# Order of the scores and of the mask on the diagonal of a causal attention kernel

## What is computed

```python
x = x + attention(layernorm(x))      # x: 2 x 2048 x 512
x = x + moe_ffn(layernorm(x))        # 8 experts of width 352, the 2 best of each token, and a shared expert
# attention, 16 heads of width 32:
k_lat = (x @ wk_w + wk_b) @ wkl_w + wkl_b      # latent width 128, then up to heads; v alike
scores = einsum('bhqd,bhkd->bhqk', q, k) / sqrt(32)
scores = where(causal, scores, -inf)
out = einsum('bhqk,bhkd->bhqd', softmax(scores), v)
```

## Time and profile before

| | us |
|---|---|
| median of 3 runs | 2658.76 |
| lowest and highest | 2655.09, 2663.19 |
| the profiled execution, its own time | 2654.73 |
| its span, first to last instruction | 2652.8 |
| mean granted TensorE clock | 0.935 |
| busy: TensorE, its weight loads, VectorE, ScalarE, GpSimd | 2338.7, 1478.8, 1560.3, 1053.6, 999.8 |
| attention (296.51 to 1484.15) | 1187.64 |

### The profile page before, as it was taken

How to read it: one execution, slowest core, us unless ns; L and a number is a source line. 1 busy time by engine, 2 the same in 40 slices (tenths; PEclk the granted TensorE clock), 3 DMA queues, 4 the chain that set the end, 5 groups by cost and what they waited for, 6 DMA issues and landing times. The chain is left out here.

```text
span 2652.8 us, 34530 instructions
## 1 busy us (share of the span) xinstructions
PE 2338.7 (88%) x12088; PEld 1478.8 (56%) x12088; DVE 1560.3 (59%) x3220; ACT 1053.6 (40%) x1928; POOL 999.8 (38%) x592
## 2 busy tenths in 40 slices
PE   5997699999999999999999699999489999999950
PEld 5775344444444444444443377776467777777740
DVE  3664787667676777766674444443645555555535
ACT  2332155565555555555656422221033333333310
POOL 0000067474656566573746633130221111112036
PEclk8998599899999999998999899999589999999975
DMA  3766512213131313322110234341245454545349
GB/s 100 279 234 231 124 28 65 65 49 74 39 81 33 82 31 80 102 65 65 49 47 27 63 105 143 111 143 48 69 151 178 139 171 146 167 154 160 113 157 381
DMA packets 178740, 301.72 MB, mean 114 GB/s; under 512 B 23616, under 2 KB 65728, under 8 KB 178624
## 3 DMA queue, kind: packets, MB, share of 16 engines
q1 hardware_dynamic: 159360, 242.54, 30.1%
q0 software_dynamic: 14656, 49.29, 5.9%
q10 hardware_dynamic: 4608, 8.39, 0.8%
HBM read 199.65 MB, written 100.27 MB: 113 GB/s over the span
## 5 line engine op out<-in xcount | busy, mean ns | idle before, releaser
L832 ACT ACTIVATE b_pt<-b_st 128x512 f32<-128x512 f32 (+3 forms) x1280 | 620.8, 533 | 489.3 <-PE b_st L910 208.3
L773 DVE TENSOR_REDUCE b_mpart<-b_mx 128x1 f32<-128x512 f32 x768 | 510.2, 685 | 209.2 <-PE b_mx L889 207.4
L649 POOL TENSOR_TENSOR b_acc<-b_acc,b_pt 128x1024 f32<-128x1024 f32 (+1 forms) x256 | 593.4, 2344 | 73.3 <-ACT b_pt L832 73.0
L910 PE MATMUL b_st<-b_q,b_k 97*128 97x512 f32 (+2 forms) x1280 | 497.9, 405 | 71.9 <-ACT b_pt L832 57.9
L889 PE MATMUL b_mx<-b_k,b_q 96*128 96x512 f32 (+2 forms) x1280 | 514.5, 418 | 30.7 <-DVE b_mt L781 25.9
L889 PEld LDWEIGHTS b_mx<-b_k,b_q 96*128 96x128 f32 x1280 | 250.4, 197 | 306.7 <-DVE b_mpart L773 138.6
L910 PEld LDWEIGHTS b_st<-b_q,b_k 97*128 97x128 f32 x1280 | 244.2, 193 | 262.9 <-ACT b_pt L832 228.7
L923 PE MATMUL b_ob<-b_pt,b_v 128*32 128x512 f32 (+3 forms) x2560 | 305.7, 550 | 1.1 <-ACT b_pt L832 1.1
L770 DVE CUSTOM_DVE_ANT_0 b_unread<-b_mx,b_later 128x384 bf16<-128x384 f32 (+3 forms) x512 | 244.6, 483 | 77.9 <-PE b_mx L889 77.4
L649 POOL TENSOR_TENSOR b_acc<-b_pt 128x1024 f32<-128x1024 f32 x48 | 113.4, 2378 | 443.8 <-ACT b_pt L832 443.7
L61 PE MATMUL e_fb<-e_xh,e_w_guh 128*128 128x512 f32 (+1 forms) x552 | 219.6, 398 | 1.5 <-DVE e_xl L1730 1.5
(11 more groups left out here) (224 smaller groups left out, 3524.2 us busy)
## 6 DMA issues: line engine op xcount, KB each, us to landing
scr_y<-e_y SPq DMA_DIRECT2D x23, 1024.0 KB, 5.0
b_q<-scr_qh SPq DMA_DIRECT2D x64, 256.0 KB, 4.4
b_k<-scr_kh SPq DMA_DIRECT2D x64, 256.0 KB, 4.0
e_gu<-in_L_ffn_w_gate_dram SPq DMA_DIRECT2D x23, 704.0 KB, 6.4
e_gu<-in_L_ffn_w_up_dram SPq DMA_DIRECT2D x23, 704.0 KB, 7.7
e_d<-in_L_ffn_w_down_dram SPq DMA_DIRECT2D x23, 512.0 KB, 7.7
a_xin<-in_L_attn_x_dram POOLq DMA_DIRECT2D x8, 1024.0 KB, 5.9
scr_qh<-a_qh SPq DMA_DIRECT2D x8, 1024.0 KB, 4.6
```

The source lines that it names most:

```text
L649: g.tensor_tensor(out[:, :, lo:], so_far[:, :, lo:], pt[n % NPB][:, :, lo:], ALU.add).then_inc(s_add, 1)
L773: v.tensor_reduce(part, mxb[i % NMX][:, 0:w], AX.X, ALU.max).then_inc(s_red, 1)
L832: act.activation(pt[n % NPB][:, j, lo:], stb[:, (2 * n + j) % NST, lo:], ACT.Exp, scale=SCALE).then_inc(s_exp, 1)
L910: pe.matmul(stb[:, (2 * n + j) % NST, lo:], kb[:, h, at:at + P], qb[:, h, q * CH + lo:(q + 1) * CH], start=True, stop=True).then_inc(s_st, 1)
```

## The change

On TensorE, in steps on the diagonal alone, the second score is issued right behind the first, before the first third of the items. On VectorE the mask is put ahead of all the maxima of its step. Waits, counts, shapes and buffers stay as they are.

```diff
@@ VectorE's loop
                 for n in range(NS):
-                    here, _, some, there = item_shares(n)
-                    for i in range(here, some):
-                        if stream[i][0] == "max":
-                            partial_max(i)
+                    here, _, _, there = item_shares(n)
                     if steps[n][2] >= TPC * steps[n][1]:
                         mask(n)
-                    for i in range(some, there):
+                    for i in range(here, there):
                         if stream[i][0] == "max":
                             partial_max(i)
@@ TensorE's loop
                 for n in range(NS):
                     here, *some = item_shares(n)
+                    diag = steps[n][2] >= TPC * steps[n][1]
                     score(n, 0)
+                    if diag:
+                        score(n, 1)
                     for i in range(here, some[0]):
                         item(i)
                     if n % 2 == 0 and n >= 4:
...
                     for i in range(some[0], some[1]):
                         item(i)
-                    score(n, 1)
+                    if not diag:
+                        score(n, 1)
                     for i in range(some[1], some[2]):
                         item(i)
```

## The result

The changed kernel takes 2703.1 us (median of 4 runs, 2699.2 to 2705.96), the kernel before 2660.98 on the same chip (4 runs, 2655.09 to 2669.25): a ratio of 1.0155, with 95% from 1.0126 to 1.0184. It is slower by 42 us where 10 were forecast (2669 against 2658.76), and lies 5 us above the range. The profiled execution took 2701.65 us, its span 2699.7, at a mean granted clock of 0.926 (0.935 before).

The account below looks back on a forecast made before the run. Diagonal steps were taken to be bound by the loop score, mask, exponential, next score. To the profiled 2654.73 us it added 0 from the walk against the trace and 12 for gaps, giving 2667, set at 2669; range 2640 to 2698.

Parts of the forecast that it names:

- the loop over the second score: Diagonal steps: second score, mask, first exponential, next second score; 1.3 to 1.6 us a turn, not shortened by the change.
- its bound of 20 us: VectorE on diagonals: masks late behind maxima, about 20 us over attention, the most the mask's move could give.
- some half of them: +12 us: Small TensorE gaps the walk left out, hidden where TensorE waits on diagonals; about half counted, adding 12 us.
- The walk: Step-by-step timing of diagonal units in both orders; over eight head groups 0 us against the trace, 22 walk against walk.
- step 1 of q=2: Transposes and ScalarE's copy ahead of the exponentials hold the loop; unit 0.4 us later against the trace, 0.9 with gaps.
- The clock rival: Longer diagonal stalls lower the granted clock: 37 to 45 us slower, 2691 to 2700, attention mean under 0.97; chance 0.14.
- The unpiling rival: q=0 step 2 turn with two products falls from 3.31 to 2.2 us; kernel 16 us faster, 2641; chance 0.20.
- A q=1 diagonal of 14 us or more: Sign for the forecast: a q=1 diagonal takes 14 us or more instead of 13.3.
- VectorE's wait for items above 193.5: Sign for the forecast, in the list of waits: VectorE's wait for items rises above 193.5 us.
- Turns 0 and 1 shorter: Sign for the forecast: on diagonals, the turns between second scores in steps 0 and 1 get shorter.
- Turns 3, 5, 7 longer: Sign for the forecast: on diagonals, the turns of steps 3, 5 and 7, those with a value product, get longer.
- TensorE's wait for exponentials above 228.7: Sign for the forecast: TensorE's wait for exponentials, 228.7 us for weight loads of scores before, rises.

Follow-up runs that it names:

- run 3: Changed kernel with the value or ones product moved behind all items of the step on the diagonal: 2640.84 us, 0.9913 of the kernel before.
- run 6: Kernel before with only VectorE's mask put first, in diagonal steps with under three items ahead of the second score: 2648.07 us, 0.9958.
- run 7: Changed kernel with ScalarE's copy of a turned row put behind the exponentials in diagonal steps: 2682.9 us, 1.0079 of the kernel before.
- run 9: Changed kernel with the product behind all items and ScalarE's copy behind the exponentials, in diagonal steps: 2637.81 us, 0.9899 of the kernel before.
- run 5: Changed kernel with the change kept in odd diagonal steps alone, the old order in even ones: 2828.35 us, 1.0644 of the kernel before.
- run 1: Changed kernel with VectorE's mask back behind the maxima of the first two thirds, so TensorE's half alone: 2973.41 us, 1.1149 of the kernel before.
- run 10: Kernel before, on diagonals: product behind the items' second third, mask first where under three items stand ahead, ScalarE's copy behind the exponentials: 2672.39 us, 1.0044.
- run 12: Kernel before with only the product moved, on the diagonal, behind the second third of the items, right ahead of the second score: 2632.5 us, 0.9876.

## Why the prediction was wrong

**Right: where and which way.** Nothing but diagonals got longer (off them attention is 7.5 us shorter), the loop over the second score stayed the bound, and the mechanism is the one forecast: "the product follows the score at once, VectorE idles over it, and the items behind it deliver their maxima just before the next mask". The 0.82 us of VectorE's wait and the mask 0.80 us behind its score show it, and run 3 tests it: put the product behind the items, change nothing else, and 2703 becomes 2641. VectorE's half stayed inside its bound of 20 us: run 6, which has it in all but eleven steps, measured 11 (1 - 0.9958 of 2660).

**Wrong: the term "some half of them: +12 us".** The walk gave 0 us against the trace and 22 against itself, and I took half of the gaps as hidden. The undisturbed units measured 29, and the clock, which the forecast's sum had at nothing, some 14 more (21 on the diagonals less 7.5 off them). So 12 should have been 43. (The sum has a slip too: 12 on 2654.73 and the 4 us of the median make 2671, not 2669.) The q=1 unit's second scores, from the first one:

- walk, new order: 0, 1.95, 3.97, 6.11, 7.77, 9.64, 11.18, 12.87, 14.61
- measured: 0, 1.96, 4.25, 6.33, 8.26, 10.04, 11.71, 13.45, 15.57

The unit is 1.6 us longer than the trace before (13.99), not 0.6. The walk misses 0.96 us, in the turns that end at scores 2, 4, 6 and 8 (0.27, 0.27, 0.13, 0.38); the four others are within 0.1. Those are turns in which TensorE's own queue sets the end. The first of them runs from 815.39 to about 817.68, without a wait inside: 0.34 + 0.21 + 0.99 + 0.57 + 0.18. The walk had 0.24 + 0.12 + 1.0 + 0.48 + 0.18 = 2.02. The reasoning "hidden where it is waiting" was wrong in its place: the gaps come behind the wait, where TensorE has just become late, and there each counts in full. In the walk's terms the sum should have been the whole 22 us or more; the undisturbed units made 29: 1.6 in q=1 for its 1.1, 1.1 in q=2 for 0.9, and 0.9 in q=3 and q=0 together for 0.7.

**Wrong: step 1 of q=2.** The prediction saw that "the transposes of the turn in step 1 and ScalarE's copy in front of that step's exponentials hold the loop", and priced the whole unit at +0.4 us against the trace (0.9 walk against walk). It measured +1.1 (16.34 against 15.21), and with the clock's part +24 us over the eight. Run 7 puts 8 us on this one copy at a clock of 1.00, and 10 at the same mean clock of the span. What the walk did not do is follow the transposes as an item: with the second score, the product and items ahead of them, they came later in the step than before, and the copy, and so two exponentials, with them.

**The clock rival came in by half.** Its mark was a clock mean under 0.97 in attention: it is 0.95. Some 21 us of the diagonals' 50 are in units with a lowered clock, less the 7.5 that came back elsewhere. But it was placed wrongly: not the stretches behind q=1 diagonals were hit most, as in the earlier trace rows, but the q=2 diagonals themselves (six of eight), and a spell in one cost 3.1 us (19.46 against 16.34) instead of 5. The q=2 diagonal is where the new order had put the longest stall, and run 7, which shortens the stall, brings four of those six q=2 units back to 1.00. That the stall decides where the clock falls fits this; how often it falls did not change with it (mean 0.95 in attention in both), and no run held the stall and changed only the clock. The Trainium skill, "TensorE: Matmul & The Clock Gate", Part 1 on the clock gate, says that sustained activity is what releases the clock. The profiled executions do not contradict it: the mean clock of the span is lower where the diagonals are longer, 0.941 in run 9 (diagonals 468.6 us), 0.934 in run 3 (476.2), 0.926 in the changed kernel (532.9), 0.895 in run 5 (618.4), 0.852 in run 1 (752.8). But a lower clock makes a diagonal longer too, so these pairs do not show which came first.

**The unpiling rival** was real, and the change hardly collected it. In the q=0 unit at 932 us the turn with the closing product is 2.67 us instead of 3.31, where the rival had 2.2, and the turns that end in steps 5 to 7 are longer by 0.23, 0.49 and 0.26. An undisturbed q=0 unit gained 0.3 us, and one with a clock of 0.71 took the gain away again (145.8 against 142.4 summed). Run 3 collects 9.5 us in q=0, about the rival's 8 x 1.1.

**The signs to look for.** A q=1 diagonal of 14 us or more: 14.9. VectorE's wait for items above 193.5: 207.4. Turns 0 and 1 shorter: the first (1.96 against 2.27), not the second (2.29 against 1.99). Turns 3, 5, 7 longer: those ending at scores 4 to 8 all are, the last by 0.78 (2.12 against 1.34), because two products and an item stand in it. TensorE's wait for exponentials above 228.7: that row, of the weight loads, fell to 194.2. The row of the matmuls, which the prediction didn't look at, rose from 57.9 to 71.7, and in the q=1 unit from 1.84 to 2.99. The sign was right in what it meant and tied to the wrong row.

**Open.** How much of the 42 us is the clock's own, since order and clock changed together; 14 is the difference that the undisturbed units leave. Whether the longer stalls bring the clock down. Why four executions of run 7 kept more of it. Which of run 10's two additions costs more. Whether run 9 or run 12 is the better one (their intervals overlap).

## What to carry to other kernels

In a queue taken in order, put independent work right ahead of an instruction that must wait, not right behind it: with the same instructions, the product behind the wait gave 2703 us and ahead of the next one 2641, and moved one place in the old order, to right ahead of the waiting score, it brought 1.2%. Order within a step is a matter of what each other engine can do meanwhile; here the items had to go first, since they feed the engine that is idle during the product. When a loop's link is moved earlier, look at every in-order copy or mask that shares a queue with the loop, and at each place where the early position ends, for the turn there holds the work of two. And read a wait from the engine that does the work: the weight loads' idle time fell here while the kernel got slower, and that of the matmuls rose.

## What had not been expected of the hardware

A matmul whose weight load had waited for a semaphore holds up the one behind it longer: 0.34 us from the score at 815.39 to the item at 815.73, against 0.23 between like instructions in an unbroken row (813.67 to 813.90), and the first one behind a product's eight does so too (0.34, from 797.49 to 797.83, before the change). It is 0.1 us each time. The turn from 815.39 has three places where the walk had 0.1 less (0.34 for 0.24, 0.21 for 0.12, 0.57 for 0.48), which make its 0.27 us; that such places make the rest of the missing 0.96 us of a unit was not followed up.
